# Edge attributes and masks of a graph convolution in four buffers, not two

## The reference

```python
def _egnn_conv(x, src, dst, edge_attr, W_msg, W_edge, W_root, b):
    msg = x[src] @ W_msg + edge_attr @ W_edge
    agg = jax.ops.segment_max(msg, dst, num_segments=x.shape[0])
    agg = jnp.where(jnp.isneginf(agg), 0.0, agg)
    return agg + x @ W_root + b
c1 = jax.nn.leaky_relu(_egnn_conv(X, src, dst, edge_attr, W1_msg, W1_edge, W1_root, b1))
c2 = jax.nn.leaky_relu(_egnn_conv(c1, src, dst, edge_attr, W2_msg, W2_edge, W2_root, b2))
```

## Time and profile before

| | us |
|---|---|
| median of 3 runs | 2445.17 |
| lowest and highest run | 2443.11, 2458.22 |
| the profiled execution | 2459.85 |
| its span, first to last instruction | 2458.0 |
| PE busy in the span | 2008.4 (82%) |
| DVE busy | 1213.8 (49%) |
| POOL busy | 822.1 (33%) |
| ACT busy | 581.9 (24%) |

### The profile page before, as it was taken

The page is one execution under the profiler, slowest core; times in us unless marked ns, Lnnn a source line. Parts: engine busy times, 40 slices in busy tenths (PEclk is TensorE's granted clock), DMA queues, the critical chain, the costliest instruction groups (busy, mean ns, idle before and its releaser), DMA issues. The chain is left out here.

```text
span 2458.0 us, 46254 instructions
## 1 busy us (share of the span) xinstructions
PE 2008.4 (82%) x18497; PEld 1659.2 (68%) x18497; DVE 1213.8 (49%) x3354; ACT 581.9 (24%) x1505; POOL 822.1 (33%) x742
## 2 busy tenths in 40 slices
PE   3688468888888438888888629999999999999868
PEld 3588435554555325554545429999999999999758
DVE  6935535565555325555555474444444444445435
ACT  4843201111111101111111123333233332332131
POOL 6433266666764346676766320000000000000000
PEclk9889679999989668999999859999999999999879
DMA  2034334554454234444444500000000000000000
GB/s 70 1 91 110 103 93 129 132 134 128 124 130 119 71 75 131 133 130 123 125 130 131 134 15 2 2 2 1 2 2 2 2 2 2 2 2 2 1 3 21
DMA packets 145659, 160.47 MB, mean 65 GB/s; under 512 B 42813, under 2 KB 130245, under 8 KB 145070
## 3 DMA queue, kind: packets, MB, share of 16 engines
q1 hardware_dynamic: 93165, 81.77, 12.4%
q0 software_dynamic: 22128, 34.74, 7.3%
q10 hardware_dynamic: 30152, 41.02, 4.6%
HBM read 101.66 MB, written 55.75 MB: 64 GB/s over the span
## 5 line engine op out<-in xcount | busy, mean ns | idle before, releaser
L1130 POOL DMA_INDIRECT c_gathered<-messages,idx_all x624 | 656.6, 1052 | 313.0 <-issue 169.6
L1163 PE MATMUL c_taken<-c_hot,rows 125*96 125x512 f16 x1300 | 520.9, 401 | 27.3 <-issue 26.7
L1162 PE MATMUL c_taken<-c_hot,rows 125*96 125x512 f16 x1300 | 523.5, 403 | 23.1 <-issue 21.9
L764 PE MATMUL l_ps<-rows,counts 125*128 125x192 f16 x5625 | 471.4, 247 | 64.9 <-DVE rows L808 64.8
L764 PEld LDWEIGHTS l_ps<-rows,counts 125*128 125x128 f16 x5625 | 466.9, 98 | 68.3 <-issue 64.4
L764 PE MATMUL l_ps<-l_u,counts 125*128 125x192 f16 x5625 | 470.3, 247 | 8.0 <-DVE l_uf L828 4.5
L764 PEld LDWEIGHTS l_ps<-l_u,counts 125*128 125x128 f16 x5625 | 467.8, 98 | 9.2 <-DVE l_uf L828 4.8
L1200 DVE TENSOR_SCALAR c_hot<-c_offset_srcs 125x512 f16<-125x512 f16 x1300 | 300.9, 292 | 257.8 <-PE c_taken L1163 113.8
L1254 ACT ACTIVATE c_back<-c_tr 128x384 f32<-128x384 f32 x208 | 101.7, 489 | 851.7 <-PE c_tr L1171 333.4
L1210 DVE TENSOR_TENSOR_SCAN c_scanned<-c_mask,c_scanned,c_msg 96x512 f32<-96x512 bf16 x156 | 198.7, 1274 | 195.8 <-DMA running_max<-c_back 62.6
L828 DVE SCALAR_TENSOR_TENSOR l_uf<-l_ps,l_cf,l_wide 125x96 f32<-125x96 f32 x400 | 127.1, 318 | 328.4 <-ACT l_wide L783 328.4
(11 more groups left out here) (255 smaller groups left out, 1515.1 us busy)
## 6 DMA issues: line engine op xcount, KB each, us to landing
running_max<-c_back ACTq DMA_DIRECT2D x208, 192.0 KB
c_attr<-attr_halves SPq DMA_DIRECT2D x412, 64.0 KB
c_mask<-segment_mask SPq DMA_DIRECT2D x206, 96.0 KB
c_gathered<-messages,idx_all POOLq DMA_INDIRECT x624
l0a_raw<-in_ea_t SPq DMA_DIRECT2D x34, 195.3 KB
c_srcs<-sources SPq DMA_DIRECT2D x50, 128.0 KB
attr_halves<-l0a_hi SPq DMA_DIRECT2D x34, 97.7 KB
attr_halves<-l0a_lo SPq DMA_DIRECT2D x34, 97.7 KB
```

The costliest lines, as they stand in the source:

```text
L764: last = pe.matmul(ps[:, t % HB, 0:2 * F], at[:, k, t * P:t * P + 128], u[hop % 2][:, k, :], start=(k == 0), stop=(k == T - 1))
L1130: pool.indirect_dma_start(out=gat[:, i % 2, j, :], out_offset=None, in_=c["y_d"], in_offset=bass.IndirectOffsetOnAxis(ap=idx_all[:, i * IT ...
L1162: pe.matmul(bank_of(i, GG), y[:, t, 0:F], one_hot, start=(t == 0), stop=False)
L1163: last = pe.matmul(bank_of(i, GG), y[:, t, F:2 * F], one_hot, start=False, stop=False)
```

## The change

`attr` and `mk` get four buffers, one for each group of a turn, with a semaphore each. Their loads wait for the group four before, not two before. The request for the sources moves from behind group 3 to behind group 2, and asks for those of turn i + 1, not i + 2. On DVE, chunk 2 of the next turn's one-hots moves from ahead of scan 3 to behind it. The numbers of instructions on each engine and of transfers stay as they were.

```diff
-        attr = sb("attr", [AE, 2, GW], F16)
-        mk = sb("mask", [F, 2, GW], BF16)
+        attr = sb("attr", [AE, GT, GW], F16)
+        mk = sb("mask", [F, GT, GW], BF16)
...
-        s_ea, s_mk, s_st = ([sem(f"{tag}_{n}{k}") for k in range(2)] for n in ("ea", "mk", "st"))
+        s_ea, s_mk = ([sem(f"{tag}_{n}{g}") for g in range(GT)] for n in ("ea", "mk"))
+        s_st = [sem(f"{tag}_st{k}") for k in range(2)]
...
                 def load_group(i, g, width):
                     n = i * GT + g
-                    k = g % 2
-                    sp.wait_ge(s_msg, n + (GT - 1))
+                    sp.wait_ge(s_msg, n + 1)
                     for q in (0, AE // 2):
-                        sp.dma_start(attr[q:q + AE // 2, k, 0:width], halves_v[:, n * GW:n * GW + width]).then_inc(s_ea[k], 16)
-                    sp.wait_ge(s_scan, n + (GT - 1))
-                    sp.dma_start(mk[:, k, 0:width], c["mask_d"][:, n * GW:n * GW + width].to_broadcast([F, width])).then_inc(s_mk[k], 16)
+                        sp.dma_start(attr[q:q + AE // 2, g, 0:width], halves_v[:, n * GW:n * GW + width]).then_inc(s_ea[g], 16)
+                    sp.wait_ge(s_scan, n + 1)
+                    sp.dma_start(mk[:, g, 0:width], c["mask_d"][:, n * GW:n * GW + width].to_broadcast([F, width])).then_inc(s_mk[g], 16)
...
                     for g in range(GT):
                         load_group(i, g, LEFT if i == last_it and g == GT - 1 else GW)
-                    if i + 2 < N_IT:
-                        load_srcs(i + 2, LEFT if i + 2 == last_it else GW)
+                        if g == 2 and 0 < i < last_it:
+                            load_srcs(i + 1, LEFT if i + 1 == last_it else GW)
...
                 def edges(i, g, start):
-                    k = g % 2
-                    pe.wait_ge(s_ea[k], 64 * i + 32 * (g // 2) + 32)
-                    return pe.matmul(bank_of(i, g), we[:, :], attr[:, k, :], start=start, stop=not start)
+                    pe.wait_ge(s_ea[g], 32 * i + 32)
+                    return pe.matmul(bank_of(i, g), we[:, :], attr[:, g, :], start=start, stop=not start)
...
-                    v.wait_ge(s_mk[k], 32 * i + 16 * (g // 2) + 16)
+                    v.wait_ge(s_mk[g], 16 * i + 16)
...
-                    v.tensor_tensor_scan(scanned[0:F, k, :], mk[:, k, :], bank_of(i, g),
+                    v.tensor_tensor_scan(scanned[0:F, k, :], mk[:, g, :], bank_of(i, g),
...
                     scan(i, 2)
-                    one_hots(i + 1, 0, 1, 2)
+                    one_hots(i + 1, 0, 1)
                     scan(i, 3)
-                    one_hots(i + 1, 3)
+                    one_hots(i + 1, 2, 3)
```

## The result

The changed kernel took **2424.61 us** (4 runs, 2414.01 to 2426.24) where the kernel before took 2446.84 us (4 runs): ratio **0.9892**, 95% interval 0.9849 to 0.9936. The forecast was 2425 us. The profiled execution of after took 2425.24 us around a span of 2423.4, so its span is 34.6 us shorter than that of before, whose own execution lay above its median.

The account below looks back on a forecast made before the run. POOL was taken to set most turns: twelve gathers and a pause of about 2 us. Attributes -15 and the tail -4, all else 0, say -20 us from a median of 2445.17, gave 2425 us; range 2380 to 2468.

Parts of the forecast that it names:

- The signs: In the convolutions: attribute waits under 5 us, fewer POOL waits for PE, turns of 17.9 to 18.6 us, longest gathers near 2.0.
- pauses without a name: POOL pauses whose releaser the trace can't name; forecast to stay at 40 or more, about 2 us each.
- The bound: In most convolution turns POOL sets the cycle: twelve gathers and a pause of about 2 us, as PE's count is seen late.
- rival A: In the convolutions PE sets the pace, so POOL's pauses go too; 82 us off, 2363 us; chance 0.23.
- Attributes: Four attribute buffers in the convolutions remove all 70.6 us of PE's waits, worth -15 us; bounds 0 and 70.6.
- One-hots: DVE's new one-hot order: 0 us, as gathers caught by two runs of six lose about as much; bounds -55 and +20.
- rival C: In the turns both runs of six one-hots lengthen gathers, mean 1.15 us; 30 us more, 2475 us; chance 0.13.
- Tail: Behind each convolution's last gather, where PE runs alone, attribute waits go: -4 us, bounds 0 and -8.8.
- First turns unchanged: The first turn of each convolution begins from the same requests; a change in its 44 us would count against the prediction.
- Masks and sources: Four mask buffers remove 11.3 us of DVE waits, worth 0 (bound -11.3); sources asked for later, behind group 2, cost 0.
- The sum: Whole kernel: -15 for attributes and -4 behind the last gathers, -19, say -20 us, so a median of 2425 us.
- The page's rule: Whichever of DVE and POOL starts first holds the shared port for one instruction; the prediction held a gather's 1.59 us against it.

Follow-up runs that it names:

- split: Changed kernel, with conv 1 gathering only in its first two turns and conv 2 using the old one-hot order; 2324.93 us, ratio 0.9515 to the kernel before.
- pause_b: Kernel before with POOL filling a private tile behind every four gathers; 2439.40 us against 2444.77, ratio 0.9984.
- bufs: Kernel before with four buffers for attributes and masks, sources and one-hots as before; 2241.25 us against 2242.81, ratio 0.9986.
- attr4: Kernel before with four buffers for the attributes alone; 2243.28 us against 2242.81, ratio 1.0004.
- srcs: Kernel before with only the request for the sources moved behind group 2; 2240.74 us against 2242.81, ratio 0.9997.
- broken_a: Changed kernel with DVE ending each chunk of one-hots before it begins the next; 2242.54 us, ratio 0.9986 to the kernel before.
- before_again: Kernel before, unchanged, run again for a trace on a chip at the lower level; 2242.02 us, one run.
- hots: Kernel before with only chunk 2 of the one-hots moved behind scan 3; 2273.79 us against 2242.81, ratio 1.0141.

## Why the prediction was right, step by step

- **The signs.** Those named for "right" came: no wait for attributes behind the first products, 6 of POOL's pauses for PE in place of 26, 41 pauses without a name of 2.05 us, turns of 18.17 and 17.93 us, longest gathers of 2.14 and 1.81 us.
- **The bound.** Shown in part. That the lateness comes with gathering was a reading of one pause; split and pause_b show it. That the turn is POOL's, twelve gathers and a pause of about 2 us, isn't shown: in pause_b the 39 us of fills between pauses cost nothing, and behind the first turns of before, after and pause_b PE never waits for gathered rows. It fits as well that PE sets the pace, held up while POOL gathers. That is the first half of rival A; its second half, that the pauses go once PE is ahead, failed (41 of them). No run parts these two.
- **Attributes: all 70.6 us of waits go, worth 15.** The waits went. Their value was mis-sized: the most that POOL's waits for PE could give was put at 30.4 us, with 6 new pauses without a name, and half of it taken. POOL's pauses fell from 129.9 to 90.7 us, 39.2, less 19 ordinary gaps of 0.30 us, 33.5 us: all of it came, and one new pause, not 6. The halving had no row behind it, only a share of PE's idle time. That all 33.5 us belong to the buffers is a reading; the trace has the whole change.
- **One-hots: 0.** At this level gathers took 583 us for 551 before (1.058 us each) and 591 for 547 after (1.080): 12 us worse, inside the bounds. The reason I gave for 0, that both runs of six are caught, was the reason for a loss: the old order's runs of three cost next to nothing, and its nine were often not one run, since chunk 2 waits for PE. The row of 637 to 646 us that I priced it from was one of 23 runs of nine in 50 turns. Where POOL never pauses, this is rival C in full: I had 30 us and a mean gather of 1.15 us, measured are 31 us and 1.04.
- **Tail: -4.** From the end of the last gather to the end of the last edge product it is 31.8 and 30.7 us before, 30.4 and 22.9 after: 9.2 us less, just past the bound of 8.8. The mechanism was wrong for most of it. Conv 1, which had the wait of 4.36 us there, gave 1.4 us; conv 2, which had no wait for attributes there, gave 7.8, because PE had less left to do when POOL ended.
- **First turns unchanged.** Conv 1's fell from 43.71 to 39.02 us, which I had named as a sign against me; conv 2's went from 38.75 to 39.08. PE's idle time in the first is about the same (18.8 and 18.2 us, and 304 to 344 us of after); its busy time differs, 25.2 and 21.8. The granted clock fell to the lower of its two levels (1.2 GHz) while PE stalled between products, at 319.2 us before and 318.7 after, and rose to the upper (2.4 GHz) at 346.5 and 339.2, after PE had run on; a product of 512 columns took 0.63 us at the lower and 0.38 at the upper. Why PE ran on sooner I can't say. In pause_b the first turns took 39.29 and 31.43 us, so one pair of traces doesn't tell a change here.
- **Masks and sources: 0.** bufs against attr4, 2 us apart, and srcs show nothing at the lower level; at the upper they weren't tried alone.
- **The sum.** -33.5 + 12 - 9 - 4.5 = -35, as the spans say (34.6), where the forecast had -15 + 0 - 4 = -19. The medians differ by 22.2 us, since the profiled execution of before lay 13 us above the median of its four runs and that of after less than 1. So the median was met partly by luck: too small a gain from the attributes stood against no loss from the one-hots, and the rest that was too small went with an execution that was slower than most. The sizes come from one pair of traces and are no surer than those 13 us.
- **What the prediction missed.** It took the profile for the kernel's own. On three of the five later chips the traces have no late counts; on one of these the changed kernel was timed, and it loses. Nothing in the trace of before could tell that.
- **The page's rule.** The prediction set the Trainium skill (SBUF — State Buffer, "Who interferes with whom") against one gather that waited 1.59 us. The page says it of vector instructions in a two-port mode, and no run shows whether the one-hots run in one. The runs agree with the row: with a rule of one instruction at a time, broken_a, which only adds gaps between chunks, would have changed nothing; it took 53 ns off the mean gather (1038 to 985).

## What to carry to other kernels

A gather on POOL that begins beside a run of such one-hots mostly waits for the end of the run, not of the instruction; beside a scan alone it didn't (0.94 us in the mean of 118 gathers in before_again). Keep such runs short, and put a chunk where the engine waits anyway. When POOL sets the pace without a pause, every 0.05 us on 624 gathers is in the time; when it pauses for something else, extra work on it can be free, as 87 us were in pause_b. Before a tuned order is changed for one per cent, the kernel before should be timed on more than one chip, since the wait that is to be removed may exist on some only.

## What the runs showed of the hardware

- The same program takes 2242 us on three chips and 2445 us on two others (and in the first comparison), 9% apart, always the same within a comparison. The difference lies where POOL gathers and PE works at once (506.3 + 507.4 us and 404.4 + 402.7); from the end of the second convolution on, where PE works almost alone, the two traces take 1063 and 1064 us. What differs between the chips is open.
- On the chips at 2445 us PE's products stall between one another without a wait in the program (1.0 to 2.2 us each in the rows shown), and its counts are seen late, by up to 7.8 us in before and 10.9 in after, most often about 2 us after POOL's last gather. In before_again, at 2242 us, no scan began more than 1.3 us late. Without gathers the turn is 14.34 us on a chip of either level. What holds PE and its counts up is open.
- A gap that is made by waiting for the end of three one-hots is enough for a gather to come in: it takes 1.18 us at most (broken_a), where it took up to 1.94 (hots).
